# Layer 1's bias row: from a matmul on TensorE to an addition on GpSimd, with two masks made later

## The reference

```
# L0, layers k = 0, 1 (mask = adj == 0)
q = x @ Wq[k].T + bq[k];  kk = x @ Wk[k].T + bk[k]
scores = where(mask, -1e10, q @ kk.T / sqrt(128))
attn = where(mask, 0, softmax(scores))
ctx = (attn @ x) @ Wc[k].T
x = layer_norm(x + ctx, ln_g[k], ln_b[k])
# L1: 8 heads of 32
h = softmax(where(mask, -inf, q_h @ k_h.T * scale)) @ v_h
y = h @ Wo + bo + x
out = (y - mean(y)) * rsqrt(var(y) + 1e-5) * gamma + beta
```

## Time and profile before

| what | value |
|---|---|
| median of 3 runs | 1209.11 us (1207.4 to 1209.9) |
| profiled execution | 1206.85 us |
| its span | 1205.1 us |
| TensorE busy | 1150.8 us, 95% |
| VectorE busy | 974.3 us, 81% |
| ScalarE busy | 926.1 us, 77% |
| GpSimd busy | 538.7 us, 45% |

### The profile page before, as it was taken

One profiled execution on the slowest core, in us unless ns is written; L12 is line 12 of the kernel. 1 busy time (PEld: TensorE's weight loads), 2 busy tenths in 40 slices (PEclk: granted clock), 3 DMA queues, 4 the chain that ended last, 5 costly groups with the idle time before them and its releaser, 6 DMA issues.

```text
span 1205.1 us, 28411 instructions
## 1 busy us (share of the span) xinstructions
PE 1150.8 (95%) x9572; PEld 839.9 (70%) x9572; DVE 974.3 (81%) x2680; ACT 926.1 (77%) x2112; POOL 538.7 (45%) x403
## 2 busy tenths in 40 slices
PE   5977999999999999999999999999999999999796
PEld 2754677777777777777777777777777777777463
DVE  4676789888888888888888888888888888888776
ACT  3235887888878788887878888787888878788774
POOL 1452344453464345346434544643453464344330
PEclk9799999999999999999999999999999999999999
DMA  8215161432615243251524325152432616122311
GB/s 242 39 36 148 29 177 35 123 89 72 158 36 161 52 123 89 68 162 36 159 53 124 89 75 154 36 169 44 123 89 75 154 37 176 36 71 72 111 31 36
DMA packets 170687, 114.06 MB, mean 95 GB/s; under 512 B 107184, under 2 KB 152240, under 8 KB 170544
## 3 DMA queue, kind: packets, MB, share of 16 engines
q1 hardware_dynamic: 168384, 104.37, 33.6%
q0 software_dynamic: 2160, 7.87, 1.9%
HBM read 61.87 MB, written 25.17 MB: 72 GB/s over the span
## 4 chain that ended last, share of the span: by engine, by line
PE 88%; DVE 3%; ACT 3%; issue 2%; POOL 1%; DMA 1%; DVEq 0%; POOLq 0%; ACTq 0%; SPq 0%
PE ps_j L798 40%; PE ps_t L811 22%; PE ps_j L915 10%; PE ps_s L790 8%; PE ps_s L784 6%; ACT probs L975 2%; PE ps_j L923 1%; DVE masked_s L1071 1%; PE ps_j L882 1%; ACT pt_h L981 0%; PE ps_j L822 0%; DMA xt<-xs 0%; DMA xt<-ys 0%; DMA x<-x_dram 0%; DMA out_dram<-y_f 0%
## 5 line engine op out<-in xcount | busy, mean ns | idle before, releaser
L1071 DVE CUSTOM_DVE_ANT_0 masked_s<-ps_s,mask 128x512 f32<-128x512 f32 x640 | 425.1, 682 | 23.8 <-PE ps_s L790 22.3
L975 ACT ACTIVATE probs<-masked_s,nm_h 128x512 f32<-128x512 f32 x512 | 367.4, 718 | 69.2 <-DVE nm_h L1071 62.3
L811 PE MATMUL ps_t<-ident,probs 128*128 128x128 f32 x2560 | 390.8, 276 | 11.0 <-ACT pt_h L981 5.5
L811 PEld LDWEIGHTS ps_t<-ident,probs 128*128 128x128 f32 x2560 | 305.1, 142 | 92.7 <-ACT probs L975 27.0
L981 ACT ACTIVATE pt_h<-ps_t 128x512 f32<-128x512 f32 x404 | 238.4, 590 | 78.3 <-PE ps_t L811 73.8
L790 PE MATMUL ps_s<-stack 128*128 128x512 f16 x512 | 194.2, 380 | 2.3 <-DVE nm_h L1071 2.3
L798 PE MATMUL ps_j<-xw,pt_l 128*128 128x256 f16 x1536 | 188.8, 274 | 0.0
L798 PEld LDWEIGHTS ps_j<-xw,pt_l 128*128 128x128 f16 x1536 | 151.2, 98 | 30.9 <-issue 0.6
L613 POOL TENSOR_TENSOR rstd_L<-var_eps_L,minus_half 128x4 f32<-128x4 f32 x32 | 32.8, 1024 | 255.4 <-DVE var_eps_L L1101 255.4
L915 PE MATMUL ps_j<-pt_h,v 128*32 128x256 f32 x2048 | 123.6, 382 | 2.9 <-DVE pt_h L1078 2.6
L1106 DVE TENSOR_TENSOR pt_l<-ps_t,pt_l 128x512 f16<-128x512 f32 x128 | 88.4, 690 | 38.3 <-ACT pt_l L981 29.1
(11 more groups left out here) (126 smaller groups left out, 1631.7 us busy)
## 6 DMA issues: line engine op xcount, KB each, us to landing
stack<-bounce SPq DMA_DIRECT2D x256, 128.0 KB, 3.1
bounce<-parts SPq DMA_DIRECT2D x64, 256.0 KB, 2.7
adj_t<-adj_dram SPq DMA_DIRECT2D x30, 512.0 KB, 5.3
x<-x_dram SPq DMA_DIRECT2D x16, 512.0 KB, 4.0
out_dram<-y_f POOLq DMA_DIRECT2D x15, 512.0 KB, 3.4
stack<-adj_dram SPq DMA_DIRECT2D x2, 512.0 KB, 5.7
pt_h<-l_wc SPq DMA_DIRECT2D x2, 256.0 KB, 4.2
xt<-ys SPq DMA_TRANSPOSE x32, 4.4
```

The source lines that it names most:

```text
L811: last = pe.transpose(ps_t[r % 2][:, t], probs[:, r, t * P:(t + 1) * P], ident[:])
L975: act.activation(probs[:, r], masked_s[:, r], ACT.Exp, bias=nm[:, n, r:r + 1], scale=-1.0, accum_out=total[:, n, r:r + 1]).then_inc(exps, 1)
L1071: dve.tensor_tensor_reduce(out=masked_s[:, r], in0=ps_s[scores_bank(pos)][:], in1=m[:, r], scale=-scale, scalar=NONE_LEFT, op0=ALU.add, op ...
```

## The change

Layer 1's bias row is no longer part of XW. Once x1 holds the normalized x with gain and shift, GpSimd writes, for each of four row tiles, `bx1` times `has_l`, a number that is 1 for a row with a neighbour and 0 for one without (four TENSOR_SCALARs of 128x256 into a scratch tile: `ot` for graphs 0 and 1, `y_l` for the others), and adds the scratch to x1 (one TENSOR_TENSOR of 128x1024). `has_l` is the minimum of the row sum and 1.0, a small reduction on VectorE in AV of layer 0. `bx1` becomes an fp32 copy. The two parts of M in a body move from tiles 29 and 32 to 33 and 34. The rest of the difference are the semaphores for this order.

```diff
-    ("M", None, "i+3", 0, (29,)),
-    ("M", None, "i+3", 1, (32,)),
+    ("M", None, "i+3", 0, (33,)),
+    ("M", None, "i+3", 1, (34,)),
...
-        bx1 = sb("bx1", [P, D], fp16)
-        mean_64 = sb("mean_64", [P, P], fp16)
+        bx1 = sb("bx1", [P, D])
...
-        sum_l = sb("sum_l", [P, 2, NT, 2])
+        sum_l = sb("sum_l", [P, 2, NT, 3])
+        has_l = sb("has_l", [P, 2, NT])
...
+            pool.memset(sum_l[:, :, :, 2:3], 1.0).then_inc(floors_in, 1)
-            pool.memset(mean_64[:], 1.0 / 64).then_inc(mean_in, 1)
...
-                pool.tensor_tensor(dst[:], dst[:], h, ALU.add).then_inc(ln_done[s], 1)
+                pool.tensor_tensor(dst[:], dst[:], h, ALU.add).then_inc(shifted if norm == 0 else ln_done[s], 1)
...
+            def add_bx(b, dst):
+
+                if early(b, 1):
+                    pool.wait_ge(bias_ready, 1)
+                    settle(pool)
+                spread = (ot[:].rearrange("p a n -> p (a n)") if early(b, 2) else y_l[:].rearrange("p t d -> p (t d)"))\
+                    .rearrange("p (t d) -> p t d", t=NT)
+                for t in range(NT):
+                    last = pool.tensor_scalar(spread[:, t], bx1[:], has_l[:, b % 2, t:t + 1], None, ALU.mult)
+                last.then_inc(bx_spread, 1)
+                pool.wait_ge(bx_spread, b + 1)
+                pool.wait_ge(shifted, b + 1)
+                pool.tensor_tensor(dst[:], dst[:], spread, ALU.add).then_inc(ln_done["L"], 1)
+
             def layer_norm_l0(b, l, dst):
                 split_y(b, l)
                 gain_and_shift("L", nth(b, l), y_l, l, dst)
+                if l == 0:
+                    add_bx(b, dst)
...
             pool.tensor_tensor(x1[:], y_f[:], shift[:, 0:1, :].to_broadcast([P, NT, D]), ALU.add)\
-                .then_inc(ln_done["L"], 1)
+                .then_inc(shifted, 1)
+            add_bx(1, x1)
             layer_norm_l0(0, 1, x2)
...
-                    if early(b, 1) and l == 1:
-                        pe.wait_ge(bias_ready, 1)
                     for t in range(2):
                         at = (2 * half + t) * P
                         last = split_product(out_bank[:, t * D:(t + 1) * D], lambda a, c: xt[:, l_buffer(b, l), a, c, at:at + P],
-                                             lambda a, c: wc0[:, a, l, c], more=l == 1)
-                        if l == 1:
-                            last = pe.matmul(out_bank[:, t * D:(t + 1) * D], mean_64[:], bx1[:],
-                                             start=False, stop=True)
+                                             lambda a, c: wc0[:, a, l, c])
...
-                    dve.tensor_scalar(bx1[:], wide[:, 0:D], UP, None, ALU.mult).then_inc(bx1_hi, 1)
-                    dve.wait_ge(bx1_hi, 1)
-                    lower = slice(P // 2, P)
-                    dve.scalar_tensor_tensor(bx1[lower], wide[lower, 0:D], UP, bx1[lower], ALU.mult, ALU.subtract)\
-                        .then_inc(bias_ready, 1)
+                    dve.tensor_copy(bx1[:], wide[:, 0:D]).then_inc(bias_ready, 1)
...
-                            dve.wait_ge(floors_in, 3)
-                        dve.tensor_reduce(some_l[:], sum_l[:, l_buffer(b, l)], ALONG, ALU.max).then_inc(some_ready, 1)
+                            dve.wait_ge(floors_in, 4)
+                        if l == 0:
+                            dve.tensor_reduce(has_l[:, b % 2], sum_l[:, l_buffer(b, l), :, 0:3:2], ALONG, ALU.min)
+                        dve.tensor_reduce(some_l[:], sum_l[:, l_buffer(b, l), :, 0:2], ALONG, ALU.max).then_inc(some_ready, 1)
```

More of the change, by code:

```diff
@@ L223, in graph_attention @@
         ident_zero, ident_in, half_in = sem("ident_zero"), sem("ident_in"), sem("half_in")
-        mean_in, bo_added, bx1_hi = sem("mean_in"), sem("bo_added"), sem("bx1_hi")
+        bo_added, shifted, bx_spread = sem("bo_added"), sem("shifted"), sem("bx_spread")
         pt_lo_ready, xw_hi = sem("pt_lo_ready"), sem("xw_hi")
@@ L961, in _ @@
             pe.wait_ge(ident_in, 1)
-            pe.wait_ge(mean_in, 1)
             program(walk)
```

## The result

The changed kernel takes 1242.14 us (median of 4 runs, 1238.58 to 1242.2), the kernel before 1208.26 us beside it. The ratio is 1.0276, with a 95% interval of 1.0258 to 1.0295: slower by 2.8%, where I had forecast 0.74%. The direction was right, the size was not, and the time lies above my range.

What follows compares the result with a forecast made beforehand. TensorE bounds the kernel unless another engine's result comes too late. Prologue 4.4 + clock 1.3 + waits at WO 10.0 - removed matmuls 6.8 = +8.9 us, on the median 1218.0 us (0.74% slower), range 1206 to 1227.

Steps and rivals of the forecast that it cites:

- What bounds it, and the place of the new wait: Loop bodies: TensorE bounds; GpSimd's longer run makes WO wait for the split of ot, 13 x 0.77 = +10.0 us.
- the formula: Loop body: its growth is GpSimd's added time, less TensorE's 0.22 us earlier arrival, less the 4.02 us usable margin.
- the duration of the spread: GpSimd, each graph: four TENSOR_SCALARs priced at 2.25 us, with the addition's 2.32 us making 4.57 us.
- Rival 2: Dear spread on GpSimd: 0.81 us per instruction, +24.2 us in all, 1233.3 us; chance 0.13.
- rival 1: Cheap spread on GpSimd at the cast's rate: 3.45 us added, no wait at WO, -2.5 us, 1206.6 us; chance 0.11.
- a lower clock behind the prologue's wait: Prologue: after about 7.1 us idle, TensorE runs at the lower clock for about 4 us, +1.3 us.
- The prologue: Spread and addition delay graph 0's layer 1 rstd by 4.4 us, all on the path; lower clock adds 1.3 us.
- Removed matmuls, 6.8 us: TensorE, bodies and prologue: 64 bias matmuls go, priced at 0.109 us each where they count; 6.8 us saved.
- TensorE waits for none of it: Loop body: VectorE has hardly a gap behind the moved masks, yet no work there holds up TensorE; zero.
- rivals 1 and 4: The fourth: GpSimd's work is hidden everywhere, 6.8 to 7.0 us faster, 1202.2 us; chance 0.05.
- The masks at zero: VectorE in the bodies: moving the two masks makes nothing wait; zero in the sum.
- the high end: Whole kernel: 1227 us, from 0.68 us per spread instruction (given as +7.6) and 2.0 us for the clock.

Runs made afterwards that it cites:

- e8: Changed kernel with a second operation (times 1.0) in the spread's TENSOR_SCALARs; 1215.16 us, ratio 1.0048.
- e10: Changed kernel with the two-operation spread and two further TENSOR_SCALARs per graph into a spare tile; 1226.35 us.
- e2: Changed kernel, spread and addition later on GpSimd: behind the split of ot in bodies, behind rstd and gain in the prologue; 1209.7 us, ratio 1.001.
- e9: Changed kernel with the addition behind the split of ot in bodies, prologue as in the changed kernel; 1215.8 us, ratio 1.0061.
- e16: Kernel before with every bias matmul made twice and mean_64 half as large; ratio 1.0058.
- e15: Changed kernel with two-operation spread, addition behind the split of ot, masks at tiles 0 and 2 of the next body; 1203.42 us, ratio 0.9958.
- e3: Changed kernel, bias row added once to layer 0's shift, no GpSimd work per graph, rows without a neighbour not excepted; 1209.85 us, ratio 1.0009.
- e7: Changed kernel with two-operation spread, addition behind the split of ot, masks back at 29 and 32; 1226.07 us.
- e12: Changed kernel with two-operation spread, addition behind the split of ot, masks at tiles 6 and 7 of the next body; 1224.43 us.
- e5: Kernel before with only the two masks moved to 33 and 34; ratio 1.001.

## Why the prediction was wrong

- **What bounds it, and the place of the new wait: right.** The run of GpSimd from rstd to the split of ot, tied to TensorE, a usable margin of 4.02 us, 13 waits, none in the 14th body (69.86 us, its 0.38 earlier). With the measured insert the formula gives 1.78 us a body, measured 1.77. The wait that it gives, 6.02 + 0.22 - 4.02 = 2.22 us, is listed as 2.00.
- **The step that failed: the duration of the spread.** I took L697, "the row nearest in shape and operands", because it has a pointer scalar, and put its 0.547 us on an instruction with one operation. The pointer hardly matters here (0.91 us against 0.85 with an immediate); the number of operations does. The nearest row was L669, one operation, which I set aside as "the other side" and then cut from 0.81 to 0.68 for an overlap. The probe of that form (immediate, one operation) shows 0.85 without any. The insert was 6.02 us, not 4.57: 1.45 us at 14 places, 20.3 of the 26.4 us by which the span's growth (35.3) exceeds my 8.9. Rival 2, with 0.81, was the nearest case and got 0.13; its own 1233.3 is still too low. The argument of rival 1, cheaper because it has one operation instead of two, was the wrong way round.
- **A term that was missing: the clock in the bodies.** I counted a lower clock behind the prologue's wait only. With waits of 2.0 us it falls in three of the twelve bodies measured, 1.63 us each, 4.9 us in all. That follows from the first error: with waits of 0.2 (e8) and 1.1 us (e10) it fell in no body. 20.3 and 4.9 leave 1.2 us, a sum of three. Ahead of the first body's WO I had forecast 5.6 us (5.7 and 0.77, less 0.88 for eight matmuls) and measured 9.76; after two spreads 1.3 are left. In these 0.7 are there before the insert begins (L738 at 83.03, L722 at 82.32), and e2, with nothing inserted there, has the same 0.77 at rstd, so they are not the insert's. From there to the thirteenth WO it is 0.8 less than the two errors give, and behind it 0.7 more than forecast.
- **The prologue: mechanism right.** 6.1 us between e9 and e2, for an insert that moves rstd by 5.8; my 4.4 + 1.3 had the smaller insert and a clock term that turns out to be partly paid in the comparison kernel already. TensorE's twelve matmuls behind the wait took 2.72 us, the 1.3 us more that I had put for them.
- **Removed matmuls, 6.8 us: price right, worth conditional.** 0.109 us each is confirmed both ways (e16, e15). But "each nanosecond of matmul taken out of a body shortens it, as long as no other engine's result comes too late" held a condition which I didn't follow up on VectorE around WO, and "TensorE waits for none of it" was wrong for nm_l. In the changed kernel this stayed unseen, because the 2 us wait for GpSimd covers it; had the insert been cheap, as in rivals 1 and 4, the kernel would have been no faster than before (e2 and e3, and e9 with the prologue's loss), not 2.5 or 7 us faster.
- **The masks at zero: right by luck.** The body is the formula's, without a term for them. But alone the move costs 0.13 us a body, which the wait at WO covers, and over the old place it saves 9.5 us in the changed kernel. I had the 0.28 us on GpSimd's side, not the 1.4 us for which VectorE stands still nor the 0.46 us by which the cast behind it is longer, nor that the clock falls in six bodies instead of three.
- **Two small slips in the figures.** 14 x 4 x 0.13 is 7.3 and not 7.6, which leaves the high end at 1227. Rival 2's 1.09 us seems to count 0.09 us until the next instruction, as the 2.25 us do; 3.25 - 2.25 alone is 1.00.

## What to carry to other kernels

Price an added instruction by a row with the same number of operations, and where rows differ by a factor, measure the form before it is placed: one spare operand was worth 27 us here. When work is taken from the bounding engine, look for the engine that comes second in that very stretch; its crowd decides whether the gain arrives. A VectorE instruction like these masks, from SBUF to SBUF, should be placed where GpSimd is idle: look for rows that are longer than their twins, since no wait is listed. Such a placement can be worth more than the work that it places.

## What was unexpected in the hardware

- GpSimd, 128x256 fp32: one operation 0.91 to 0.93 us with a pointer scalar and 0.85 with an immediate; two operations 0.47 to 0.54 and 0.41; a plain copy 0.40; multiplication of two tensors 0.73.
- A mask on VectorE (0.69 us alone) took 2.24 (e7) and 2.65 us (e12) beside a TENSOR_TENSOR of GpSimd, and ended 0.55 us behind it in both.
- After one and the same wait of TensorE the granted clock sometimes falls and sometimes not. In the kernel before, 2.73 us in the prologue left it at the upper level, and six matmuls took 0.81 us; in e5 the same wait was followed by this:

```profile
89.11 1.44 PE L798 MATMUL ps_j<-wc,xt 128*128 128x256 f16 x6 [2.73 <-DVE qt L1197]
```

Of 64 runs of the kernel before beside the experiments 35 lie between 1206.6 and 1207.8 us, with a mean granted clock of 0.990 or 0.991 in all but one, and 29 at 1208.8 us or more, with 0.987 to 0.989 in all but four. That this is the same fall is likely, but is not shown run by run.
